# Second cross attention: one burst of four value-product groups per head in place of two bursts of two

## The chip, the cores and the metric

The kernel is one program on one core of a Trainium2 chip. The metric is device time in microseconds (us), the median of the runs; lower is better. The engines are TensorE (PE in the rows; its weight loads are PEld), VectorE (DVE), ScalarE (ACT), GpSimd (POOL) and SyncE (SP, which issues the DMAs).

## The reference

A two-layer perceiver block: in each layer a cross attention from 256 query rows to 4096 context rows, a self attention, and a feed-forward. The change lies in the cross attention of the second layer, with 16 heads of 16 columns and D = 256:

```python
def _L1_xattn_ref(query, key, value, mask, Wq, bq, Wk, bk, Wv, bv, Wo, bo):
    q = _split_heads(query @ Wq.T + bq)
    k = _split_heads(key @ Wk.T + bk)
    v = _split_heads(value @ Wv.T + bv)
    scores = jnp.einsum('bhqd,bhkd->bhqk', q, k) / jnp.sqrt(jnp.float32(DK))
    scores = jnp.where(mask, scores, jnp.float32(-1000000000.0))
    p = jax.nn.softmax(scores, axis=-1)
    out = jnp.einsum('bhqk,bhkd->bhqd', p, v)
    out = out.transpose(0, 2, 1, 3).reshape(query.shape[0], -1, D)
    return out @ Wo.T + bo
```

The mask is all true here, so the kernel takes its branch without masking.

## The kernel before

`stage_cross1` does this attention, from about 375 to 563 us of the span. One head follows another; `pairs_of_heads` runs heads 0 and 1 in straight code, heads 2 to 13 in a loop of six rounds of two heads, and heads 14 and 15 in straight code again. The order of each engine's work is written out by hand; semaphores tie the engines together.

A head has these kinds of work:

- **Score products** (`qk`, L1506): eight groups of four products each, keys by queries, 128x1024 per group, in two PSUM places that alternate. ScalarE takes the exponential of a group (L1412) into `probs`; a group may start when the exponential of the group two before it is done.
- **Value products** (`pv`, L1522): for each of the eight groups four float32 products that add into one PSUM bank, `ACC_BANK`. The four use 32 columns of the array each and lie side by side on the partitions 0, 32, 64 and 96. A float32 product has two records in the trace, so a group is two passes of four records. Here `pv g` is the value products of group g.
- **Block products** (`m_scores`, L1476): the same scores in the other layout, queries by keys, 16 blocks of 128x512 for the row maxima of a *later* head. VectorE reads each block with a maximum over the keys (L1631). They are numbered here M0 to M15 by their place in a head: M0 to M11 belong to the next head, M12 to M15 to the one after it.
- **Reduction** (`sel`, L1532): two small float32 products that add the four parts of the previous head's accumulator; VectorE then takes the reciprocal (L1640) and multiplies (L1642). The row maxima go through L1635 to GpSimd, come back by a turn on TensorE (`m_turn`, L1490) and are copied by ScalarE (L1424) into the score operand.

The block products share three PSUM banks with `sel`, which takes one of them once per head. So from M3 on a block product waits until VectorE has read the block three places before it:

```python
bank_before = {0: -2, 1: -1, 2: -3, 3: 0, 4: 2, 5: 3, 6: 1}.get(idx, idx - M_BANKS)
...
pe.wait_ge(s["m_read"], n_m * h + bank_before + 1)
```

VectorE's order in a head is: the reads of M0 to M11, L1635, L1640 and L1642 (which wait for `sel`), then the reads of M12 to M15. TensorE's order, from M0 on, is: M0, qk 0, M1 to M3, qk 1, M4, qk 2, M5, **pv 0 and 1**, M6, qk 3, M7 to M9, qk 4, M10, qk 5, M11, **pv 2 and 3**, `sel` of the head before, M12, qk 6, M13, qk 7, M14, M15, pv 4 and 5, `m_turn`, pv 6 and 7, then M0 of the next head. In heads 14 and 15 block products that would belong to heads past the last are left out: head 14 has no M12 to M15, head 15 none at all. Head 0 has no `sel` behind it.

Of the kernel before, what the change touches and what calls it, by code (L numbers as in the profile page):

```python
# [295 lines left out]
def transpose_rows(k, src, banks, done):  # L296

    for t in range(QT):
        for c in range(KT):
            last = k.nc.tensor.transpose(k.ps[:, banks, c * S + t * P:c * S + (t + 1) * P],  # L300
                                         src[:, t, c * P:(c + 1) * P], k.ident[:, :])
    last.then_inc(done, 1)
# [632 lines left out]
def rows_linear(k, src, n_k, w, bias, bank, done):  # L935

    t = k.nc.tensor
    for q in range(QT):
        o = k.ps[:, bank, q * D:(q + 1) * D]
        for c in range(n_k):  # L940
            last = t.matmul(o, src[:, c, q * P:(q + 1) * P], w[:, c, :], start=(c == 0),  # L941
                            stop=(bias is None and c == n_k - 1))
        if bias is not None:
            last = t.matmul(o, k.ones_row[0:1, 0:P], bias, start=False, stop=True)
    last.then_inc(done, 1)


def keep_busy(k, n, bank, cols=2 * D):

    for _ in range(n):  # L950
        k.nc.tensor.matmul(k.ps[:, bank, 0:cols], k.ones_sq[:, :], k.w1_o[:, :, :].rearrange("p t n -> p (t n)")[:, 0:cols], start=True, stop=True)  # L951
# [338 lines left out]
def stage_cross1(k):  # L1290
# [45 lines left out]
    with nc.Block() as block:  # L1336
# [98 lines left out]
        def _(pe):  # L1435
            t = nc.tensor

            def turn_first():

                for h in range(2):  # L1440
                    for q in range(QT):
                        last = t.transpose(turned(ACC_BANK)[:, (h * QT + q) * P:(h * QT + q + 1) * P],
                                           k.q_rows1[:, q * 2 + h, :], k.ident_bf[:, :])
                last.then_inc(s["q_turned"], 1)
# [12 lines left out]
            def m_scores(it, b, idx, masked, first, begin=False):  # L1457

                h = 2 * it + b
                blk, q = divmod(idx, QT)  # L1460
                quarter = idx // 4
                if idx == 0 and begin:
                    pe.wait_ge(s["q_first"], 1)
                elif idx == 0:
                    pe.wait_ge(qm_in[b], 16 * it)
                if idx % 4 == 0:
                    pe.wait_ge(k_in[b][quarter], 16 * K_LOADS1 * (it + 1))
                bank_before = {0: -2, 1: -1, 2: -3, 3: 0, 4: 2, 5: 3, 6: 1}.get(idx, idx - M_BANKS)
                if idx == 2 and not begin and not (first and b == 0):
                    pe.wait_ge(s["o_read"], h - 2)  # L1470
                elif not (begin and b == 0 and idx < 3):
                    pe.wait_ge(s["m_read"], n_m * h + bank_before + 1)
                o = k.ps[:, m_bank(m_turn_of(idx)), :]
                key0 = (blk % (m_blocks // 2)) * 512
                qs = k.q_st if first and h < 2 else k.q_m
                last = t.matmul(o, qs[0:MAXROW, b, q * P:(q + 1) * P],  # L1476
                                k.k_st[0:MAXROW, 2 * b + blk // (m_blocks // 2), key0:key0 + 512], start=True, stop=not masked)
                if masked:
                    last = t.matmul(o, k.ident_bf[:, :], k.mask_bias[:, q, blk * 512:(blk + 1) * 512], start=False, stop=True)
                last.then_inc(s["m_scores"], 1)  # L1480
# [34 lines left out]
            def pv(h, b, g, first):  # L1515
                pe.wait_ge(s["exp"], groups * h + g + 1)
                if g == 0:
                    pe.wait_ge(s["v_staged"], h + 1)
                    if not first:
                        pe.wait_ge(s["acc_copied"], h)  # L1520
                for m in range(GROUP_CH):
                    last = t.matmul(k.ps[32 * m:32 * m + 32, ACC_BANK, 0:S], k.v_st[:, b, GROUP_CH * g + m, :], probs[:, g, m, :],  # L1522
                                    start=(g == 0), stop=(g == groups - 1))
                last.then_inc(s["pv"], 1)
# [11 lines left out]
            def all_heads(masked):  # L1536
                keep_busy(k, 4, 6, D)
                pe.wait_ge(k.sem("c_aq"), 1)
                o = k.ps[:, 2, :].bitcast(BF16)
                for q in range(QT):  # L1540
                    for c in range(KT):
                        last = t.transpose(o[:, c * S + q * P:c * S + (q + 1) * P], k.a_q[:, q, c * P:(c + 1) * P], k.ident_bf[:, :])
                last.then_inc(k.sem("c_aqT_ps"), 1)
                pe.wait_ge(k.sem("c_aqT"), 1)
                rows_linear(k, k.a_qT, KT, k.w_tern, None, 3, k.sem("c_y"))
                keep_busy(k, 5, 6)
                pe.wait_ge(k.sem("c_xn"), QT)
                transpose_rows(k, k.xn, 2, k.sem("c_xnT_ps"))
                pe.wait_ge(k.sem("c_xnT"), 1)
                rows_linear(k, k.xnT, KT, k.w1_q, None, 3, k.sem("d_q"))  # L1550
                keep_busy(k, 2, 6)
                pe.wait_ge(s["rows"], 1)
                turn_first()
                for idx in range(n_m):
                    m_scores(0, 0, idx, masked, True, True)
                    if idx in (10, 13):
                        turn(2 * (idx // 3) - 6)
                        turn(2 * (idx // 3) - 5)
                for idx in range(M_AHEAD):
                    m_scores(0, 1, idx, masked, True, True)  # L1560
                pe.wait_ge(s["q_stack"], H // 4)
                m_turn(0, 0, True)

                def body(it, first, last):
                    for b in range(2):
                        h = 2 * it + b
                        behind = not (first and b == 0)
                        before = behind and not (first and b == 1)

                        def m_some(n0, n1):  # L1570
                            for x in m_beside(it, b, n0, n1, last):
                                m_scores(*x, masked, first)

                        if behind:
                            pv(h - 1, 1 - b, groups - 2, not before)
                            pv(h - 1, 1 - b, groups - 1, not before)
                        m_some(0, 1)
                        qk(it, b, 0, masked, first)
                        m_some(1, 4)
                        qk(it, b, 1, masked, first)  # L1580
                        m_some(4, 5)
                        qk(it, b, 2, masked, first)
                        m_some(5, 6)
                        pv(h, b, 0, not behind)
                        pv(h, b, 1, not behind)
                        m_some(6, 7)
                        qk(it, b, 3, masked, first)
                        m_some(7, 10)
                        qk(it, b, 4, masked, first)
                        m_some(10, 11)  # L1590
                        qk(it, b, 5, masked, first)
                        m_some(11, 12)
                        pv(h, b, 2, not behind)
                        pv(h, b, 3, not behind)
                        if behind:
                            if last and b == 1:
                                sel(h - 1, 1 - b, n_m * H, H - 2)
                            else:
                                sel(h - 1, 1 - b, n_m * (h + 1) + n_m - 2, None)
                        m_some(12, 13)  # L1600
                        qk(it, b, 6, masked, first)
                        m_some(13, 14)
                        qk(it, b, 7, masked, first)
                        m_some(14, 16)
                        pv(h, b, 4, not behind)
                        pv(h, b, 5, not behind)
                        if not (last and b == 1):
                            m_turn(*((it, 1) if b == 0 else (it + 1, 0)))

                pairs_of_heads(pe, body)  # L1610
                for g in range(groups - 2, groups):
                    pv(H - 1, 1, g, False)
                keep_busy(k, 1, 2, D)
                sel(H - 1, 1, n_m * H, H - 1)
                keep_busy(k, 1, 2, D)
# [499 lines left out]
```

## Time and profile before

| | before |
|---|---|
| median of 3 runs | 720.36 us (720.25 to 722.64) |
| profiled execution, span | 715.4 us |
| TensorE busy | 612.3 us (86%) |
| ScalarE busy | 456.7 us (64%) |
| VectorE busy | 407.2 us (57%) |
| one head of the loop, M0 to the next M0 | 11.91 us |

The span is the time from the first to the last instruction of one profiled execution; the median of the runs lies 5.0 us above it, outside the span. Busy times are shares of the whole span, over stages with different limits. Within the stage the change touches, a TensorE row's duration covers the whole flight of a product, and products overlap, so the row's start, and the distance to the next start, tells more than its busy time.

### The profile page before, as it was taken

How to read it: one execution, taken by the hardware profiler on the slowest of the kernel's cores; microseconds unless marked ns; L12 is line 12 of the kernel's file. 1: busy time of each engine (PE TensorE's matmuls, PEld its weight loads, DVE VectorE, ACT ScalarE, POOL GpSimd, SP SyncE). 2: the span in 40 equal slices, each digit the busy share in tenths (PEclk: the TensorE clock that was granted, in tenths of full speed). 3: DMA queues.
4: the chain of work that ended last, by engine and by line, in shares of the span. 5: the costliest groups of instructions: out<-in, count | busy, mean ns of one | idle time of the engine just before them, and what ended most of it. 6: DMA issues, size and time to landing. Idle time of an engine off the chain costs nothing. (4 is left out here: it accounts for less than half of the span.)

```text
span 715.4 us, 14402 instructions
## 1 busy us (share of the span) xinstructions
PE 612.3 (86%) x4946; PEld 365.9 (51%) x4946; DVE 407.2 (57%) x899; ACT 456.7 (64%) x541; POOL 67.4 (9%) x151
## 2 busy tenths in 40 slices
PE   1698858878878879795679999999999999898998
PEld 0353424444444445463435555555555575574786
DVE  6567371322223134876389898989896226645644
ACT  3889969999999994683027676767676414603111
POOL 3000101100001100101031212121211000000000
PEclk9999989999999999999789999999999999999999
DMA  5786766556534313203602333332231390000000
GB/s 133 217 241 228 215 198 194 146 182 188 155 103 113 92 44 99 66 2 110 199 3 79 84 80 83 80 84 78 83 80 29 101 297 1 2 1 1 0 1 15
DMA packets 52832, 73.46 MB, mean 103 GB/s; under 512 B 10979, under 2 KB 29731, under 8 KB 52795
## 3 DMA queue, kind: packets, MB, share of 16 engines
q1 hardware_dynamic: 52027, 72.25, 34.8%
q10 hardware_dynamic: 768, 0.73, 0.4%
q8 instruction: 23, 0.38, 0.2%
q14 instruction: 14, 0.11, 0.1%
HBM read 58.90 MB, written 12.85 MB: 100 GB/s over the span
## 5 line engine op out<-in xcount | busy, mean ns | idle before, releaser
L1631 DVE TENSOR_REDUCE sb_m_blk<-ps 128x1 f32<-128x512 f32 x256 | 159.5, 684 | 18.9 <-PE ps L1476 17.7
L1412 ACT ACTIVATE sb_probs<-ps 128x1024 f32<-128x1024 f32 x128 | 125.8, 1024 | 50.0 <-PE ps L1506 49.7
L655 ACT ACTIVATE sb_probs<-ps 128x1024 f32<-128x1024 f32 x128 | 124.0, 1016 | 15.8 <-PE ps L701 13.4
L659 ACT ACTIVATE sb_probs<-sb_probs,sb_neg_cap,sb_cap 128x4096 f32<-128x4096 f32 x32 | 121.6, 3801 | 1.1
L718 PE MATMUL ps<-sb_probs,sb_v_st 128*32 128x256 f32 x1024 | 76.5, 395 | 39.5 <-ACT sb_probs L659 36.8
L701 PE MATMUL ps<-sb_q_st,sb_k_st 112*128 112x256 bf16 x512 | 75.7, 283 | 5.8 <-DMA sb_k_st<-k_parts_l 3.6
L1506 PE MATMUL ps<-sb_q_st,sb_k_st 115*128 115x256 bf16 x512 | 76.4, 272 | 1.5 <-ACT sb_probs L1412 1.5
L1476 PE MATMUL ps<-sb_k_st,sb_q_m 96*128 96x512 bf16 x224 | 76.6, 383 | 0.0
L701 PEld LDWEIGHTS ps<-sb_q_st,sb_k_st 112*128 112x128 bf16 x512 | 46.0, 100 | 48.9 <-ACT sb_probs L655 24.1
L1522 PE MATMUL ps<-sb_probs,sb_v_st 128*32 128x256 f32 x1024 | 67.4, 384 | 0.2 <-ACT sb_probs L1412 0.2
L718 PEld LDWEIGHTS ps<-sb_probs,sb_v_st 128*32 128x32 f32 x1024 | 24.0, 110 | 68.0 <-ACT sb_probs L659 45.0
L1506 PEld LDWEIGHTS ps<-sb_q_st,sb_k_st 115*128 115x128 bf16 x512 | 48.7, 97 | 18.0 <-issue 1.4
L1522 PEld LDWEIGHTS ps<-sb_probs,sb_v_st 128*32 128x32 f32 x1024 | 31.3, 109 | 27.3 <-issue 14.3
L951 PE MATMUL ps<-sb_w_o,sb_ones_sq 128*128 128x512 f32 (+1 forms) x82 | 35.3, 566 | 11.0 <-issue 11.0
L1082 ACT ACTIVATE sb_q_all<-ps,sb_nmax 128x256 f32<-128x256 f32 (+1 forms) x72 | 31.7, 452 | 12.1 <-DVE sb_nmax L1098 12.1
L1476 PEld LDWEIGHTS ps<-sb_k_st,sb_q_m 96*128 96x128 bf16 x224 | 22.7, 101 | 30.0 <-DVE sb_m_blk L1631 17.1
L613 POOL TENSOR_TENSOR sb_v_st<-sb_v_rows,sb_keep 128x512 f32<-128x512 f32 x14 | 14.9, 1065 | 210.8 <-PE ps L718 142.6
L861 DVE RECIPROCAL sb_rec<-ps 128x2 f32<-128x2 f32 x16 | 2.7, 170 | 51.5 <-PE ps L727 51.5
L855 DVE COPY sb_acc_sb<-ps 128x256 f32<-128x256 f32 x16 | 6.8, 423 | 41.5 <-PE ps L718 41.5
L1098 DVE TENSOR_REDUCE sb_nmax<-ps 128x2 f32<-128x512 f32 (+1 forms) x36 | 22.6, 631 | 13.5 <-PE ps L1021 7.2
L1073 ACT ACTIVATE sb_q_all<-ps 128x512 f32<-128x512 f32 (+1 forms) x36 | 19.8, 551 | 15.6 <-PE ps L1034 15.4
L1929 ACT ACTIVATE sb_probs<-ps 128x512 f32<-128x512 f32 x9 | 5.4, 597 | 36.9 <-PE ps L1887 36.9
(282 smaller groups left out, 824.0 us busy)
## 6 DMA issues: line engine op xcount, KB each, us to landing
sb_k_st<-k_parts_l SPq DMA_DIRECT2D x223, 64.0 KB, 2.0
sb_k_st<-k_parts_l SPq DMA_DIRECT2D x93, 128.0 KB, 3.2
k_parts_l<-sb_v_proj SPq DMA_DIRECT2D x24, 256.0 KB
k_parts_l<-sb_early SPq DMA_DIRECT2D x48, 128.0 KB
sb_v_proj<-ctxT_blocks SPq DMA_DIRECT2D x8, 512.0 KB, 8.4
sb_early<-ctxT SPq DMA_DIRECT2D x7, 512.0 KB, 3.8
sb_v_rows<-ctx_by_pair SPq DMA_DIRECT2D x7, 512.0 KB, 4.2
sb_k_st<-k_parts_l SPq DMA_DIRECT2D x64, 32.0 KB, 1.8
```

The costliest lines, as they stand in the source:

```text
L655: a.activation(probs[:, j % 2, 4 * g:4 * g + 4, :], scores_bank(g), ACT.Tanh).then_inc(s["tanh"], 1)
L659: a.activation(probs[:, j % 2], probs[:, j % 2], ACT.Exp, bias=k.neg_cap[:, 0:1], scale=k.cap[:, 0:1]).then_inc(s["exp"], 1)
L701: last = t.matmul(out[:, c, :], k.k_st[0:STACK0, j, n * P:(n + 1) * P], k.q_st[0:STACK0, j // 2, :], start=True, stop=True)
L718: last = t.matmul(k.ps[32 * m:32 * m + 32, 4 + b, 0:S], k.v_st[:, b, (j % 2) * UNIT_CH + ch, :], probs[:, j % 2, ch, :], start=(j % 2 == 0 ...
L951: k.nc.tensor.matmul(k.ps[:, bank, 0:cols], k.ones_sq[:, :], k.w1_o[:, :, :].rearrange("p t n -> p (t n)")[:, 0:cols], start=True, stop=True)
L1082: sc.activation(k.sp_rows[:, n % 2, e, 0:nk], a.scores(n)[:, e, 0:nk], ACT.Exp, bias=k.nmax[:, 2 * n + e:2 * n + e + 1], accum_out=k.sums[ ...
L1098: v.tensor_reduce(k.nmax[:, 2 * n:2 * n + 2], a.scores(n)[:, :, 0:nk], AX.X, ALU.max, negate=True).then_inc(s["max"], 1)
L1412: sc.activation(probs[:, g], scores_bank(g), ACT.Exp).then_inc(s["exp"], 1)
L1476: last = t.matmul(o, qs[0:MAXROW, b, q * P:(q + 1) * P], k.k_st[0:MAXROW, 2 * b + blk // (m_blocks // 2), key0:key0 + 512], start=True, st ...
L1506: last = t.matmul(out[:, c, :], k.k_st[0:STACK, j, ch * P:(ch + 1) * P], k.q_st[0:STACK, b, :], start=True, stop=not masked)
L1522: last = t.matmul(k.ps[32 * m:32 * m + 32, ACC_BANK, 0:S], k.v_st[:, b, GROUP_CH * g + m, :], probs[:, g, m, :], start=(g == 0), stop=(g = ...
L1631: v.tensor_reduce(k.m_blk[:, b, q, blk:blk + 1], k.ps[:, m_bank(m_turn_of(idx)), :], AX.X, ALU.max).then_inc(s["m_read"], 1)
```

## The change

The value products of groups 0 and 1 leave their place between M5 and M6 and stand ahead of those of groups 2 and 3, between M11 and `sel`. M6 follows M5 directly. Nothing is added or taken away, and no wait is written differently.

```diff
                         qk(it, b, 2, masked, first)
-                        m_some(5, 6)
-                        pv(h, b, 0, not behind)
-                        pv(h, b, 1, not behind)
-                        m_some(6, 7)
+                        m_some(5, 7)
                         qk(it, b, 3, masked, first)
                         m_some(7, 10)
                         qk(it, b, 4, masked, first)
                         m_some(10, 11)
                         qk(it, b, 5, masked, first)
                         m_some(11, 12)
-                        pv(h, b, 2, not behind)
-                        pv(h, b, 3, not behind)
+                        for g in range(4):
+                            pv(h, b, g, not behind)
                         if behind:
```

In program order on TensorE, head 14 of before, from M4 on (L1476 is a block product, L1506 a score product, L1522 a value product; x8 is two groups). The heads of the loop have the same sequence with register instructions between:

```order
L1476 MATMUL ps<-sb_k_st,sb_q_m 128x512
L1506 MATMUL ps<-sb_q_st,sb_k_st 128x256 x4
L1476 MATMUL ps<-sb_k_st,sb_q_m 128x512
L1522 MATMUL ps<-sb_probs,sb_v_st 32x256 x8
L1476 MATMUL ps<-sb_k_st,sb_q_m 128x512
L1506 MATMUL ps<-sb_q_st,sb_k_st 128x256 x4
L1476 MATMUL ps<-sb_k_st,sb_q_m 128x512 x3
```

The same place, changed, from qk 1 on:

```order
L1506 MATMUL ps<-sb_q_st,sb_k_st 128x256 x4
L1476 MATMUL ps<-sb_k_st,sb_q_m 128x512
L1506 MATMUL ps<-sb_q_st,sb_k_st 128x256 x4
L1476 MATMUL ps<-sb_k_st,sb_q_m 128x512 x2
L1506 MATMUL ps<-sb_q_st,sb_k_st 128x256 x4
L1476 MATMUL ps<-sb_k_st,sb_q_m 128x512 x3
```

The value products between M5 and M6 are gone; M5 and M6 are neighbours. Later in the same head, before, from qk 4 to `sel` (L1532):

```order
L1506 MATMUL ps<-sb_q_st,sb_k_st 128x256 x4
L1476 MATMUL ps<-sb_k_st,sb_q_m 128x512
L1506 MATMUL ps<-sb_q_st,sb_k_st 128x256 x4
L1476 MATMUL ps<-sb_k_st,sb_q_m 128x512
L1522 MATMUL ps<-sb_probs,sb_v_st 32x256 x8
L1532 MATMUL ps<-sb_quad_sum,sb_acc_sb 128x32 x2
```

And changed:

```order
L1506 MATMUL ps<-sb_q_st,sb_k_st 128x256 x4
L1476 MATMUL ps<-sb_k_st,sb_q_m 128x512
L1506 MATMUL ps<-sb_q_st,sb_k_st 128x256 x4
L1476 MATMUL ps<-sb_k_st,sb_q_m 128x512
L1522 MATMUL ps<-sb_probs,sb_v_st 32x256 x16
L1532 MATMUL ps<-sb_quad_sum,sb_acc_sb 128x32 x2
```

All four groups now stand between M11 and `sel`. VectorE's order is the same in both kernels.

## Rows read from the trace of the kernel before

**Rows 1.** The page, part 1: busy us and share of each engine.

```profile
PE 612.3 (86%) x4946; PEld 365.9 (51%) x4946; DVE 407.2 (57%) x899; ACT 456.7 (64%) x541; POOL 67.4 (9%) x151
```

**Rows 2.** Stretches: length, busy of PE, PEld, DVE, ACT, POOL; clock, DMA share, GB/s.

```profile
469.82:481.73 11.91, 11.91 (x119) 6.63 (x119) 10.46 (x19) 8.41 (x10) 1.81 (x6) 1.00 0.32 82
...
20.00:35.00 15.00, 9.57 (x85) 5.66 (x84) 6.46 (x10) 12.04 (x8) 0.00 (x0) 1.00 0.88 243
```

**Rows 3.** Waits, heads 2 to 13: who for whom: us, times, longest.

```profile
PEld ps L1476 <- DVE sb_m_blk L1631: 14.7, 36, 0.4
DVE sb_m_blk L1631 <- PE ps L1476: 13.2, 12, 1.2
```

**Rows 4.** TensorE's timeline over one head: start us, us, instruction, count.

```profile
469.82 0.39 PE L1476 MATMUL ps<-sb_k_st,sb_q_m 96*128 96x512 bf16 x1
...
472.32 0.38 PE L1476 MATMUL ps<-sb_k_st,sb_q_m 96*128 96x512 bf16 x1
472.63 1.07 PE L1522 MATMUL ps<-sb_probs,sb_v_st 128*32 128x256 f32 x16
473.63 0.39 PE L1476 MATMUL ps<-sb_k_st,sb_q_m 96*128 96x512 bf16 x1
473.86 0.60 PE L1506 MATMUL ps<-sb_q_st,sb_k_st 115*128 115x256 bf16 x4
474.30 0.90 PE L1476 MATMUL ps<-sb_k_st,sb_q_m 96*128 96x512 bf16 x3
...
475.48 0.38 PE L1476 MATMUL ps<-sb_k_st,sb_q_m 96*128 96x512 bf16 x1
...
476.13 0.38 PE L1476 MATMUL ps<-sb_k_st,sb_q_m 96*128 96x512 bf16 x1
476.44 1.07 PE L1522 MATMUL ps<-sb_probs,sb_v_st 128*32 128x256 f32 x16
477.44 0.63 PE L1532 MATMUL ps<-sb_quad_sum,sb_acc_sb 128*128 128x32 f32 x4
...
479.75 1.28 PE L1522 MATMUL ps<-sb_probs,sb_v_st 128*32 128x256 f32 x19
...
481.73 0.39 PE L1476 MATMUL ps<-sb_k_st,sb_q_m 96*128 96x512 bf16 x1
```

**Rows 5.** The same timeline in narrow stretches: second and fourth pass of a burst.

```profile
472.87 0.61 PE L1522 MATMUL ps<-sb_probs,sb_v_st 128*32 128x256 f32 x8
...
473.30 0.40 PE L1522 MATMUL ps<-sb_probs,sb_v_st 128*32 128x256 f32 x4
```

**Rows 6.** Timeline of the weight loads: M9's, with its idle time and releaser.

```profile
474.81 0.10 PEld L1476 LDWEIGHTS ps<-sb_k_st,sb_q_m 96*128 96x128 bf16 x1 [0.41 <-DVE sb_m_blk L1631]
```

**Rows 7.** VectorE's timeline, the head's twelve reads, and from narrow stretches single starts.

```profile
470.25 7.55 DVE L1631 TENSOR_REDUCE sb_m_blk<-ps 128x1 f32<-128x512 f32 x12 [1.10 <-PE ps L1476]
...
472.11 1.28 DVE L1631 TENSOR_REDUCE sb_m_blk<-ps 128x1 f32<-128x512 f32 x2
472.71 1.28 DVE L1631 TENSOR_REDUCE sb_m_blk<-ps 128x1 f32<-128x512 f32 x2
...
474.06 0.69 DVE L1631 TENSOR_REDUCE sb_m_blk<-ps 128x1 f32<-128x512 f32 x1
474.72 1.29 DVE L1631 TENSOR_REDUCE sb_m_blk<-ps 128x1 f32<-128x512 f32 x2
...
478.12 0.17 DVE L1640 RECIPROCAL sb_rec<-ps 128x2 f32<-128x2 f32 x1
```

**Rows 8.** Timelines of ScalarE and TensorE in the last head, head 15.

```profile
554.48 1.95 ACT L1412 ACTIVATE sb_probs<-ps 128x1024 f32<-128x1024 f32 x2
...
557.86 0.61 PE L1506 MATMUL ps<-sb_q_st,sb_k_st 115*128 115x256 bf16 x4 [0.68 <-ACT sb_probs L1412]
558.40 1.07 PE L1522 MATMUL ps<-sb_probs,sb_v_st 128*32 128x256 f32 x16
559.40 0.63 PE L1532 MATMUL ps<-sb_quad_sum,sb_acc_sb 128*128 128x32 f32 x4
```

## The prediction, made before the changed kernel was run

> **What bounds the kernel now.** I read the page first, then the stretch of one head, then its waits, then the timelines of TensorE and VectorE side by side. The page gives TensorE as the busiest engine [rows 1], and the stretch of one head goes further: TensorE busy for all of its 11.91 us, VectorE for 10.46, ScalarE for 8.41, at a granted clock of 1.00 [rows 2]. The reader should not stop there. A product's row covers its flight, so short waits between products vanish in it, and VectorE at 88% is close enough to matter by stretches. The waits show both engines held by each other in every head: the weight loads of the block products wait for VectorE's reads 36 times in twelve heads, and VectorE waits for a block product once per head [rows 3].
>
> The timelines say where. VectorE reads M0 to M11 in one run of 7.55 us without an idle gap that the row shows, from 470.25 to 477.80, and the only long idle time, 1.10 us, lies ahead of it, while TensorE works on the value products of groups 4 to 7 [rows 7, 4]. So a head has two parts. From M0 to `sel` (469.82 to 477.44, 7.62 us) TensorE hands out blocks and VectorE reads them at 0.60 us each (472.11, 472.71): TensorE can be at most three blocks ahead, because there are three banks. From `sel` to the next M0 (477.44 to 481.73, 4.29 us) TensorE works at its own pace and VectorE has time over [rows 4, 7].
>
> In the first part TensorE has little time over today. M9 is the block where it can be seen: M7 starts at 474.30, and with the spacing of two block products, 0.22 us (0.23 from M6 to the score product behind it), M9 would start at 474.74; its weights are loaded at 474.81, released by VectorE [rows 4, 6]. That is 0.07 us. It fits the read of M6, which starts at 474.06 and takes 0.69: 474.75, and 0.06 us more to reach TensorE [rows 7]. I use these 0.06 us for every such release.
>
> **What the change takes away.** A burst of value products has ends that cost time. Into the first: M5 starts at 472.32 and the burst at 472.63, 0.31 us where the next product would otherwise come after 0.22, so 0.09. The second pass starts 0.24 after the first (472.87), while the two after that take 0.43 together, 0.215 each: 0.03. Out of it: the last pass starts at 473.30 and M6 at 473.63, 0.33 where another pass would take 0.215: 0.12 [rows 4, 5]. Together 0.24 us. One burst per head less would save 0.24 x 16 = 3.8 us, if TensorE were free to use it.
>
> **What it moves.** Pv 0 and 1 leave a place where VectorE has to catch up. I walk one head with the rows' times; all up to M5 (472.32) stays as it is.
> M6: TensorE would be ready at 472.54. Its bank is that of M3, whose read starts at 472.11 and takes 0.68 (a pair of reads 1.28, less 0.60): 472.79, and 0.06: M6 starts at 472.85. Wait 0.31.
> M7: from M6 to M7, with four score products between, is 0.67 us (473.63 to 474.30): 473.52. M4's read ended at 473.39, no wait.
> M8: ready at 473.74. M5's read starts at 473.31, ends 473.99: M8 at 474.05. Wait 0.31.
> M9: ready at 474.27. M6's read now follows M5's at once: 473.91 to 474.59: M9 at 474.65. Wait 0.38, where it was 0.07.
> M10 comes 0.67 later (475.48 less 474.81), 475.32, and M11 0.65 after that, 475.97; the reads of M7 and M8 end at 475.19 and 475.79, no wait [rows 4, 6, 7].
> So with the burst of 1.00 us (472.63 to 473.63) gone from the way, M11 comes only 0.16 us earlier (it was 476.13). Behind it the burst starts after 0.31, at 476.28, with eight passes: 0.24 + 6 x 0.215 + 0.33 = 1.86. `sel` starts at 478.14 instead of 477.44: **0.70 us later**. By the other road: waits of 1.00 in place of 0.07, less the burst's ends of 0.24, is 0.69.
>
> Nothing behind `sel` gives it back. VectorE's reciprocal starts 0.68 us after `sel` (478.12) and waits for it, the reads of M12 to M15 stand behind it in VectorE's order, and TensorE's 4.29 us to the next M0 show no block product that waits [rows 4, 7]. VectorE ends the twelve reads at 477.59 instead of 477.80 (M6's at 473.91, and five more at 0.60 and 0.68 for the last) and then idles. Whoever else waits for pv 0 and 1 has time: ScalarE overwrites `probs` of group 0 only in the next head, after 482, and GpSimd waits for pv 7 alone. ScalarE's exponentials of groups 2 and 3 are done before 475, ahead of the burst. No DMA and no queue is passed.
>
> Rows at the same offsets from M0 stand in heads 2 to 13, so 12 x 0.70 = 8.4 us. In heads 1 and 14 M5 comes 0.08 later while the reads do not: 0.62 each, 1.2 us. Head 0 has no `sel`; M12 comes late instead, about 0.6. Head 15 has no blocks and is bound by ScalarE: the two exponentials from 554.48 end at 556.43, and qk 5 waits for a third; with pv 0 and 1 out of the way that one starts at 556.42, by the spacing of 0.91 to 1.02, where now the last score product of the batch waits until 557.86. Qk 5 would then start near 557.5, 0.36 earlier, and `sel` follow 0.54 + 1.86 later, at 559.9 instead of 559.40: 0.5 [rows 8]. **Sum: 8.4 + 1.2 + 0.6 + 0.5 = 10.7 us.** The profiled execution would go from 715.4 to 726.1; the median lies 5.0 us above the span, so 720.36 becomes **731.1 us**.
>
> **Bounds of what the trace does not show.** A clean burst of eight passes is not in it. From below it is the sum above, 1.86. From above it is the existing long burst of pv 4 to 7 with the turn's two products inside, 479.75 to 481.73 [rows 4]: 1.98, so 0.12 more per head, 1.9 us in all. The reads follow each other at 0.60 when the block is there, and at 0.66 behind a read that had to wait (474.06 to 474.72) [rows 7]. M9 to M11 hang on three reads; 0.06 each would be at most 0.18 per head, 2.9 us. On the other side, only M9's wait decides when M11 comes; if its release took 0 instead of 0.06, a head would gain 0.06, 1.0 us in all; and if heads 0 and 15, which I walked least closely, lost nothing, 1.1 us more. I take 0.60, 0.06 and 1.86, since these are the rows of the same instructions in the same order. With one upper bound at a time, and half a microsecond for the scatter of the median, the case by itself spans 728.5 to 734.
>
> **Rivals.**
> *TensorE keeps the saving.* If the blocks' banks were free when TensorE reaches M6, M8 and M9, only the burst's ends would count: 720.36 - 3.8 = 716.5 us, faster by 0.54%. The row for it is TensorE's full busy time beside VectorE's 10.46 of 11.91 [rows 2]. It decides at M6: M3's read would have to end by 472.48, and it ends at 472.79 in a run of reads that starts with M0's arrival and has no gap to close [rows 7]. The Trainium skill, page "TensorEngine Tiling (Array Packing)", Key Properties, says that changing the tiling mode drains the engine. The 0.24 us are how that looks here, and by that rule alone fewer switches are a gain. The same page, PSUM Bottleneck, says that tiling speeds up TensorE but not the emptying of PSUM; here the emptying is that of the untiled blocks, and by that rule the change loses. I give this rival 0.04.
> *The lost time is given back behind `sel`.* VectorE finishes M11 about 0.9 us earlier than now relative to `sel`, and if the tail of 4.29 us held a wait on the maxima's way over GpSimd and ScalarE, the head would come out at its old 11.91 us: 720.4. Against it: TensorE's rows behind `sel` follow at the spacing of their kind, and the turn inside the long burst starts without a gap [rows 4]. Half given back would be 725.7. 0.06 for no change.
> *The clock falls.* TensorE waits 0.93 us more per head. At 1.2 GHz in place of 2.4, the 7.6 us of one part of a head would take up to twice as long; in two heads that is 15 us, 746. Against it: in the first attention TensorE was busy for 9.57 of 15 us and the clock was 1.00 [rows 2]; no single wait here is over 0.4 us. 0.04.
>
> **How the numbers follow.** The forecast has 0.86, and is slower by 1.5%. About 0.5% (3.6 us) is what a measurement of this kernel can tell from no change. Faster by more than that has 0.04, the first rival; within it 0.06, the second; slower 0.90, the forecast and the clock. The range is the forecast's own, 728.5 to 734: it leaves out the rivals, 0.14, and little of its own case.
>
> **What would show it.** One head of the loop, M0 to M0, 12.6 us instead of 11.91. M6 starting about 0.53 after M5, not 0.22; M9's weight load released by VectorE with a longer idle time ahead of it. The burst behind M11 with 32 records, and from its start to `sel` 1.86 us. VectorE idle ahead of L1640, waiting for `sel`, about 1.0 us per head, where it now starts 0.3 after the last read has ended; its 1.10 us ahead of M0's read unchanged. Wrong would be: M6 at 0.22 after M5 (the banks were free), or a stretch from `sel` to M0 shorter than 4.29.

## The result

The changed kernel takes 732.51 us, median of 6 runs (731.96 to 733.28); the kernel before, run beside it, 721.86 (720.25 to 723.89). The ratio is 1.0145, 95% interval 1.0121 to 1.0169: slower by 10.65 us. The forecast was 731.1, and 10.7 slower.

| | before | changed |
|---|---|---|
| median | 721.86 us | 732.51 us |
| profiled execution, span | 715.4 us | 730.4 us |
| one head of the loop, M0 to M0 | 11.91 us | 12.60 us |
| M0 of head 1 to M0 of head 14 | 154.90 us | 163.87 us |
| head 15, first score product to `sel` | 6.75 us | 8.75 us |
| stage, first score product to last value product | 187.7 us | 199.9 us |

The spans differ by 15.0 us, more than the medians: 12.2 us lie in the stage and 2.8 us (2.05 ahead of it, 0.76 behind it) in places where both kernels are the same, which the section on the experiments takes up. The 5.0 us by which the first median of the kernel before lies above its profiled span are hardly all time outside the span. The time of that one execution is not on record, but in every run that has both, 1.7 to 3.0 us lie outside; the rest would then be that the profiled execution was a fast one.

One head of the changed kernel, in the columns of [rows 2] (length, then busy of PE, PEld, DVE, ACT, POOL; clock, DMA share, GB/s; the clock is the mean over the stretch, 1.00 being 2.4 GHz and 0.50 being 1.2 GHz):

```profile
477.29:489.89 12.60, 12.09 (x119) 6.85 (x119) 10.30 (x19) 8.31 (x10) 1.81 (x6) 1.00 0.28 77
```

TensorE has lost its unbroken busy time: 0.51 us per head are gaps now. There is one burst less, so fewer ends, and yet the head is longer; the clock is still 1.00. The waits of heads 2 to 13 answer to [rows 3]:

```profile
PEld ps L1476 <- DVE sb_m_blk L1628: 23.0, 48, 0.5
...
DVE sb_m_blk L1628 <- PE ps L1476: 13.2, 12, 1.2
DVE sb_rec L1637 <- PE ps L1532: 12.4, 12, 1.0
```

VectorE's long idle time ahead of M0's read is what it was, 13.2 us in twelve heads. New are 12 more waits of TensorE's weight loads, one more per head, and 12.4 us in which VectorE waits for `sel`, 1.03 per head. TensorE's timeline over the same head answers to [rows 4] (start, us, instruction, count):

```profile
477.29 0.39 PE L1476 MATMUL ps<-sb_k_st,sb_q_m 96*128 96x512 bf16 x1
...
479.79 0.38 PE L1476 MATMUL ps<-sb_k_st,sb_q_m 96*128 96x512 bf16 x1
480.32 0.39 PE L1476 MATMUL ps<-sb_k_st,sb_q_m 96*128 96x512 bf16 x1
480.54 0.60 PE L1506 MATMUL ps<-sb_q_st,sb_k_st 115*128 115x256 bf16 x4
480.98 0.92 PE L1476 MATMUL ps<-sb_k_st,sb_q_m 96*128 96x512 bf16 x2
482.11 0.39 PE L1476 MATMUL ps<-sb_k_st,sb_q_m 96*128 96x512 bf16 x1 [0.21 <-DVE sb_m_blk L1628]
...
482.77 0.38 PE L1476 MATMUL ps<-sb_k_st,sb_q_m 96*128 96x512 bf16 x1
...
483.43 0.38 PE L1476 MATMUL ps<-sb_k_st,sb_q_m 96*128 96x512 bf16 x1
483.74 1.93 PE L1522 MATMUL ps<-sb_probs,sb_v_st 128*32 128x256 f32 x32
485.61 0.63 PE L1532 MATMUL ps<-sb_quad_sum,sb_acc_sb 128*128 128x32 f32 x4
...
489.89 0.39 PE L1476 MATMUL ps<-sb_k_st,sb_q_m 96*128 96x512 bf16 x1
```

M5 is at 479.79 and M6, which now follows it directly, at 480.32: 0.53 later, not 0.22. The weight loads of M3, M6, M8 and M9 (answering to [rows 6]) and VectorE's rows (to [rows 7]) say why:

```profile
478.46 0.10 PEld L1476 LDWEIGHTS ps<-sb_k_st,sb_q_m 96*128 96x128 bf16 x1 [0.41 <-DVE sb_m_blk L1628]
...
480.31 0.10 PEld L1476 LDWEIGHTS ps<-sb_k_st,sb_q_m 96*128 96x128 bf16 x1 [0.50 <-DVE sb_m_blk L1628]
...
481.51 0.10 PEld L1476 LDWEIGHTS ps<-sb_k_st,sb_q_m 96*128 96x128 bf16 x1 [0.50 <-DVE sb_m_blk L1628]
482.11 0.10 PEld L1476 LDWEIGHTS ps<-sb_k_st,sb_q_m 96*128 96x128 bf16 x1 [0.50 <-DVE sb_m_blk L1628]
```

```profile
477.71 7.33 DVE L1628 TENSOR_REDUCE sb_m_blk<-ps 128x1 f32<-128x512 f32 x12 [1.10 <-PE ps L1476]
...
486.28 0.17 DVE L1637 RECIPROCAL sb_rec<-ps 128x2 f32<-128x2 f32 x1 [1.03 <-PE ps L1532]
```

Besides M3's, which waits in the kernel before too (there also with 0.41 us ahead of it), three loads of a head are released by a read, each after 0.50 us without a load. By the count of the waits only M8's is new, because M6's was put down to a read in the kernel before as well; M3's and M6's there:

```profile
471.00 0.10 PEld L1476 LDWEIGHTS ps<-sb_k_st,sb_q_m 96*128 96x128 bf16 x1 [0.41 <-DVE sb_m_blk L1631]
...
473.63 0.10 PEld L1476 LDWEIGHTS ps<-sb_k_st,sb_q_m 96*128 96x128 bf16 x1 [0.41 <-DVE sb_m_blk L1631]
```

But M6's came right behind the burst, 0.84 us after the read of M3 had ended (472.79 to 473.63): there the burst held it, and now the read does. The twelve reads shrink from 7.55 to 7.33 us, all that the earlier M6 brings; behind them VectorE stands for 1.03 us until the long burst is over and `sel` comes.

### The profile page after: what moved, and what is told of

It is laid out like the page before. It is cut to its first block and busy times, and to the rows that moved or that the text cites. A ratio compares the mean times of both kernels' runs of the same rounds, so it can differ in the third digit from the quotient of the medians.

```text
span 730.4 us, 14402 instructions
## 1 busy us (share of the span) xinstructions
PE 619.1 (85%) x4946; PEld 370.9 (51%) x4946; DVE 403.3 (55%) x899; ACT 455.0 (62%) x541; POOL 67.2 (9%) x151
## 3 DMA queue, kind: packets, MB, share of 16 engines
HBM read 58.90 MB, written 12.85 MB: 98 GB/s over the span
## 5 line engine op out<-in xcount | busy, mean ns | idle before, releaser
L1628 DVE TENSOR_REDUCE sb_m_blk<-ps 128x1 f32<-128x512 f32 x256 | 157.1, 685 | 17.8 <-PE ps L1476 17.8
L718 PE MATMUL ps<-sb_probs,sb_v_st 128*32 128x256 f32 x1024 | 75.7, 392 | 39.1 <-ACT sb_probs L659 36.7
L1476 PE MATMUL ps<-sb_k_st,sb_q_m 96*128 96x512 bf16 x224 | 80.1, 383 | 7.0 <-DVE sb_m_blk L1628 3.6
L1506 PE MATMUL ps<-sb_q_st,sb_k_st 115*128 115x256 bf16 x512 | 76.9, 273 | 1.9 <-ACT sb_probs L1412 1.9
L1522 PE MATMUL ps<-sb_probs,sb_v_st 128*32 128x256 f32 x1024 | 65.1, 388 | 0.2 <-ACT sb_probs L1412 0.2
L1506 PEld LDWEIGHTS ps<-sb_q_st,sb_k_st 115*128 115x128 bf16 x512 | 48.8, 97 | 18.6 <-issue 1.7
L718 PEld LDWEIGHTS ps<-sb_probs,sb_v_st 128*32 128x32 f32 x1024 | 23.9, 109 | 67.4 <-ACT sb_probs L659 44.9
L1522 PEld LDWEIGHTS ps<-sb_probs,sb_v_st 128*32 128x32 f32 x1024 | 33.8, 111 | 26.2 <-issue 11.0
L1476 PEld LDWEIGHTS ps<-sb_k_st,sb_q_m 96*128 96x128 bf16 x224 | 22.6, 101 | 38.7 <-DVE sb_m_blk L1628 25.6
L951 PEld LDWEIGHTS ps<-sb_w_o,sb_ones_sq 128*128 128x128 f32 x82 | 16.6, 212 | 25.4 <-issue 24.6
```

Source lines behind the costliest of these rows:

```text
L718: last = t.matmul(k.ps[32 * m:32 * m + 32, 4 + b, 0:S], k.v_st[:, b, (j % 2) * UNIT_CH + ch, :], probs[:, j % 2, ch, :], start=(j % 2 == 0 ...
L1476: last = t.matmul(o, qs[0:MAXROW, b, q * P:(q + 1) * P], k.k_st[0:MAXROW, 2 * b + blk // (m_blocks // 2), key0:key0 + 512], start=True, st ...
L1506: last = t.matmul(out[:, c, :], k.k_st[0:STACK, j, ch * P:(ch + 1) * P], k.q_st[0:STACK, b, :], start=True, stop=not masked)
L1628: v.tensor_reduce(k.m_blk[:, b, q, blk:blk + 1], k.ps[:, m_bank(m_turn_of(idx)), :], AX.X, ALU.max).then_inc(s["m_read"], 1)
```

## The experiments

The theory: three PSUM banks let TensorE be three blocks ahead; pv 0 and 1 stood where VectorE has to catch up, and moved away they uncover the waits. Rivals: the long burst costs by itself; the number and ends of the bursts decide; the times ahead of and behind the stage play in. Where a head's time is given it comes from the profile of that kernel and is the same within 0.02 us in every head of the loop, or alternates between the two values given. The single runs of the kernel before scatter more than that (715.7 to 726.4 us beside the experiments), so the ratios below are to be read with their intervals; a ratio is not always the quotient of two medians.

**The changed kernel again.** No edit.

> The changed kernel once more, for its head period and for what lies outside it. In the first profile a head of the loop took 12.60 us against 11.91, M0 of head 1 to M0 of head 14 8.97 us more, and head 15 2.0 us more in place of my 0.5, with a granted clock of 0.60 in its long burst; 2.8 us came ahead of the stage, where the code is the same. Theory: the period comes again at 12.60, the slow clock in head 15 comes again since TensorE there waits four times for an exponential, and the 2.8 us ahead of the stage do not, or come elsewhere (they are scatter of the clock in thin stretches): 10 to 12 us over the kernel before. Rival: head 15's slow clock was chance; then its first score product to sel takes about 7.3 us, not 8.75.

Median 730.40 us, ratio 1.0127 (1.0078 to 1.0176). The head takes 12.61 us, M0 of head 1 to M0 of head 14 163.89, the stage 199.9, head 15 again 8.76 us to `sel`. The first score product starts at 375.5 instead of 377.1 (375.1 in the kernel before). So what lies inside the stage came again to within 0.03 us, the slow head 15 too. Of the 2.05 us ahead of it 0.4 are left; the 0.8 behind it came again.

**Short reads, kernel before and changed kernel.** VectorE takes the maximum over 128 of a block's 512 columns.

```diff
-v.tensor_reduce(..., k.ps[:, m_bank(m_turn_of(idx)), :], AX.X, ALU.max)
+v.tensor_reduce(..., k.ps[:, m_bank(m_turn_of(idx)), 0:128], AX.X, ALU.max)
```

> The kernel before with VectorE's reads of the blocks cut from 512 to 128 columns (the maxima are then over a quarter of the keys); everything else as it was. If the reads hold TensorE only by the 0.07 us that I read at M9 and about as much at M3, a head of the loop takes about 11.75 to 11.85 us in place of 11.91, 1 to 2 us less in all. If the reads were what sets the whole head, it would be clearly shorter, about TensorE's own 11.77 or less.

> The changed kernel with the same short reads of 128 columns. Theory (the blocks' banks are what costs): the 0.69 us per head go, M6 starts 0.22 after M5. Walking on with the rows, the next thing late is the exponential: the score products of group 3 would be ready 0.44 after M5 but the exponential of group 1 lets them go 0.3 us later, and group 5 waits some 0.1 for group 3, so most of the 0.24 saved at the burst's ends is lost there: a head of 11.7 to 11.95 us, the whole kernel within 3 us of the one with short reads before, 2 us of it head 15. Rival one (TensorE alone counts): 11.53 us, 3.8 less than with short reads before. Rival two (a burst of four groups costs by itself, whatever VectorE does): 12.5 us, over 10 us more.

Before: a head takes 11.73 and 11.85 us in turn, M0 of head 1 to M0 of head 14 153.31, the stage 2.0 us less than the profile of before; median 715.81, ratio 0.9914 (0.9879 to 0.9950). Changed: 11.88 and 11.96, 154.88, median 718.72, ratio 0.9973 (0.9941 to 1.0005). The heads came as expected, and the price of the change fell from 8.97 us over thirteen heads to 1.57. Head 15 cost 0.4 us (6.75 to 7.16) where 2 were expected. The median of the first is 4 us lower than the stage explains; that part was not expected. The timeline of the changed kernel with short reads, M5 to `sel`, and its score products' weight loads:

```profile
460.48 0.60 PE L1476 MATMUL ps<-sb_k_st,sb_q_m 96*128 96x512 bf16 x2
461.21 0.61 PE L1506 MATMUL ps<-sb_q_st,sb_k_st 115*128 115x256 bf16 x4
...
463.80 1.93 PE L1522 MATMUL ps<-sb_probs,sb_v_st 128*32 128x256 f32 x32
465.66 0.63 PE L1532 MATMUL ps<-sb_quad_sum,sb_acc_sb 128*128 128x32 f32 x4
```

```profile
461.20 0.33 PEld L1506 LDWEIGHTS ps<-sb_q_st,sb_k_st 115*128 115x128 bf16 x4 [0.62 <-ACT sb_probs L1412]
...
463.04 0.22 PEld L1506 LDWEIGHTS ps<-sb_q_st,sb_k_st 115*128 115x128 bf16 x3 [0.30 <-ACT sb_probs L1412]
```

M5 and M6 stand in one row now, 0.22 apart, so the banks are no longer late. Next late is ScalarE: the score products of group 3 start 0.73 after M5 and not 0.44, released by an exponential. The long burst takes 1.86 us (1.87 in the changed kernel), so it is not what costs, and TensorE alone does not set the time either.

**Short reads and short exponentials.** In addition one of a group's four chunks goes through the exponential, the others stay stale.

```diff
-sc.activation(probs[:, g], scores_bank(g), ACT.Exp)
+sc.activation(probs[:, g, 0:1], scores_bank(g)[:, 0:1], ACT.Exp)
```

> The kernel before with VectorE's reads of 128 instead of 512 columns and ScalarE's exponentials of one of a group's four chunks (128x256 instead of 128x1024; the rest of the probabilities is stale). This takes both other engines out of TensorE's way. Expected: a head at TensorE's own pace, 11.7 to 11.8 us, and head 15 several us shorter, since the exponentials bound it.

> The changed kernel with the same short reads and short exponentials. Theory: with both waits gone the burst's ends alone are left, so the change gains what I read from the rows, 0.24 us a head: 11.5 us, 3 to 4 us less in all than with both short before. Rival (a long burst has a price of its own): no gain, or a loss.

One head of each, before first:

```profile
454.39:466.12 11.73, 11.73 (x119) 6.91 (x119) 4.76 (x19) 3.72 (x10) 1.80 (x6) 1.00 0.33 84
```

```profile
451.84:463.33 11.49, 11.49 (x120) 7.09 (x119) 4.69 (x19) 3.72 (x10) 1.81 (x6) 1.00 0.32 83
```

11.73 and 11.49 us: with both partners out of the way the change *gains* 0.24 us a head, the number read from the burst's ends. The stage is 3.8 us shorter with it (182.8 to 179.0), the medians differ by 3.1 (713.63 and 710.54; ratios 0.9852, 0.9802 to 0.9901, and 0.9832, 0.9798 to 0.9865, whose intervals overlap, so this rests on the profiles). The saving is real and was eaten. Head 15 of the first became 1.4 us shorter (6.75 to 5.34), not several.

**Same bursts, another place.** In the kernel before, pv 0 and 1 now stand between M7 and M8 (the edit is shortened here).

```diff
-m_some(5, 6); pv(h, b, 0, ...); pv(h, b, 1, ...); m_some(6, 7)
+m_some(5, 7)
 qk(it, b, 3, masked, first)
-m_some(7, 10)
+m_some(7, 8); pv(h, b, 0, ...); pv(h, b, 1, ...); m_some(8, 10)
```

> The kernel before, with pv 0 and 1 two steps later (between M7 and M8, behind qk 3) and not merged: as many bursts as before, of the same size, with the same products between. If the number and the ends of the bursts decided, nothing would change: 11.91 us a head. Theory (M6 waits for M3's read): walking with the rows, M6 starts 0.31 late, the burst of 1.00 behind M7 then covers the waits of M8 and M9, M11 starts 0.24 later than before, and a head takes 12.15 us, 3 to 3.5 us more in all.

12.15 us a head, M0 of head 1 to M0 of head 14 157.88, 3.0 us over before. Its timeline from M5:

```profile
466.39 0.38 PE L1476 MATMUL ps<-sb_k_st,sb_q_m 96*128 96x512 bf16 x1
466.93 0.39 PE L1476 MATMUL ps<-sb_k_st,sb_q_m 96*128 96x512 bf16 x1 [0.15 <-DVE sb_m_blk L1631]
...
467.59 0.38 PE L1476 MATMUL ps<-sb_k_st,sb_q_m 96*128 96x512 bf16 x1
467.90 1.07 PE L1522 MATMUL ps<-sb_probs,sb_v_st 128*32 128x256 f32 x16
468.90 0.61 PE L1476 MATMUL ps<-sb_k_st,sb_q_m 96*128 96x512 bf16 x2
...
471.75 0.63 PE L1532 MATMUL ps<-sb_quad_sum,sb_acc_sb 128*128 128x32 f32 x4
```

M6 waits as in the changed kernel (0.54 behind M5), M8 and M9 do not: the burst covers them. Not the number of bursts but what they cover decides. The timing does not show the 3 us: median 723.32 against 721.29, ratio 0.9998 (0.9971 to 1.0024). By profile the expectation held, by the timing it did not. Head 15 came out shorter in this order than in either other, 6.44 us to `sel` at a clock of 1.00, against 6.75 before; a kernel with this order in head 15 alone was not run.

**Head 15.** Four kernels. The changed one with the old order in head 15 alone; the one before with the new order there alone; that one with three idle products in the gaps; and the changed one with them. An idle product is one into a free bank whose result nobody reads. Of the idle products the edit shows the first.

```diff
 qk(it, b, 2, masked, first)      # head 15 alone; another keep_busy behind qk 3 and qk 4
+pe.wait_ge(s["m_read"], n_m * H); keep_busy(k, 1, 6, D)
```

> The changed kernel, but head 15 in the old order (pv 0 and 1 behind group 2). Theory: head 15's thin stretch, in which TensorE waits for ScalarE and has no value products to do, is what brings the clock down to 1.2 GHz for the burst behind it; with the old order the clock stays at 1.00 there and head 15 takes 6.75 us from its first score product to sel, not 8.75: 2 us less than the changed kernel, head period still 12.60. Rival (the slow clock was chance): the same as the changed kernel within 0.5 us.

> The kernel before, with the new order in head 15 alone. Theory: head 15 has no blocks, so what it loses it loses by waiting for ScalarE and by the clock: from its first score product to sel 8.75 us with a stretch at 1.2 GHz, as in the changed kernel twice, against 6.75; or 7.15, as with the short reads, if the clock holds. Everything ahead of it as before, 11.91 us a head. In all 0.4 to 2 us more, too little for the timing; the profile decides. Rival (head 15's price comes from the heads ahead of it, which wait for VectorE): 6.75 us.

> The kernel before with the new order in head 15 alone, and there one idle product of 256 float32 columns into a free bank behind each of the score products of groups 2, 3 and 4, in the time in which TensorE waits for an exponential. Theory: the clock fell in head 15 (three of three full-length runs with the new order there) because TensorE had so little to do; with the gaps filled the granted clock stays at 1.00 through the burst and head 15 takes 7.1 to 7.5 us from its first score product to sel. Rival (the long burst itself, or the place, brings the clock down): a stretch at 1.2 GHz again and 8.7 us or more.

> The changed kernel with the three idle products in head 15, a second sample of the filled gaps, now behind fifteen heads of the new order. Theory: clock 1.00 through head 15's burst, 7.2 us from its first score product to sel, 1.55 less than in the changed kernel twice; a head of the loop 12.60 us as there. Rival: it falls here too, 8.7 us.

| kernel | order in head 15 | first score product to `sel` | clock, mean |
|---|---|---|---|
| before, first profile | old | 6.75 us | 1.00 |
| old order in head 15 alone | old | 6.76 us | 1.00 |
| changed, first and second profile | new | 8.75, 8.76 | 0.80, 0.81 |
| before with new head 15 | new | 8.76 | 0.81 |
| before with new head 15, gaps filled | new | 7.19 | 1.00 |
| changed, gaps filled | new | 7.19 | 1.00 |
| changed, short reads | new | 7.16 | 1.00 |

The timeline of head 15 in the changed kernel answers to [rows 8], and three stretches of it, the last across the other two, show the clock:

```profile
566.73 0.60 PE L1506 MATMUL ps<-sb_q_st,sb_k_st 115*128 115x256 bf16 x4 [0.77 <-ACT sb_probs L1412]
567.83 0.61 PE L1506 MATMUL ps<-sb_q_st,sb_k_st 115*128 115x256 bf16 x4 [0.51 <-ACT sb_probs L1412]
568.84 0.60 PE L1506 MATMUL ps<-sb_q_st,sb_k_st 115*128 115x256 bf16 x4 [0.40 <-ACT sb_probs L1412]
569.66 1.03 PE L1506 MATMUL ps<-sb_q_st,sb_k_st 115*128 115x256 bf16 x4 [0.23 <-ACT sb_probs L1412]
570.63 3.10 PE L1522 MATMUL ps<-sb_probs,sb_v_st 128*32 128x256 f32 x32
573.66 0.63 PE L1532 MATMUL ps<-sb_quad_sum,sb_acc_sb 128*128 128x32 f32 x4
```

```profile
566.73:570.63 3.90, 2.77 (x17) 1.35 (x17) 0.00 (x0) 3.79 (x5) 0.00 (x0) 0.87 0.00 0
570.63:573.66 3.03, 3.03 (x34) 1.31 (x33) 0.00 (x0) 1.02 (x1) 0.00 (x0) 0.60 0.02 5
569.70:573.00 3.30, 3.30 (x28) 1.58 (x32) 0.00 (x0) 1.85 (x2) 0.00 (x0) 0.50 0.02 5
```

The long burst takes 3.03 us where it takes 1.87 in the heads ahead; from 569.70 to 573.00 the clock is 0.50, 1.2 GHz. Its second pass starts at 571.06, 0.43 us after the first:

```profile
571.06 1.07 PE L1522 MATMUL ps<-sb_probs,sb_v_st 128*32 128x256 f32 x7
```

TensorE had waited for an exponential ahead of four groups of score products; the value products that used to stand between them had been its work. The kernel before with the new order in head 15 alone has the same 8.76 us, so the heads ahead of it are not the cause. With the gaps filled by idle products (in the kernel before with the new head 15) the same burst runs at full clock:

```profile
550.55:555.88 5.33, 4.49 (x35) 2.90 (x31) 0.00 (x0) 4.68 (x6) 0.00 (x0) 1.00 0.00 0
555.88:557.74 1.86, 1.86 (x33) 0.93 (x32) 0.00 (x0) 1.20 (x2) 0.00 (x0) 1.00 0.04 9
```

That makes the order worth 0.4 us (6.76 to 7.19) and the clock 1.57. In three unfilled profiles the clock fell, in two filled ones it did not. In the fourth unfilled one, with short reads, it did not fall either, though its gaps in head 15 are the same. So the burst itself is not the cause, and the gaps do not always suffice; that they are needed is likely, but two filled profiles do not prove it, and what else it takes was not found. The kernel before with the new head 15 has a ratio of 1.0020 (0.9988 to 1.0052): too little for the timing, as expected. The filled kernels were timed once each, 718.66 us against 716.27 for the kernel before beside it, and 726.76 against 719.26, with 12.60 us a head in the second as expected. The old order in head 15 alone took 6.76 us there, but its stage came out at 199.8 us, no shorter than the changed kernel's, because head 0 ran 1.9 us longer at a low clock; its median of 730.52 shows no gain.

**The kernel before again.**

> The kernel before once more, for its profile. The stage took 12.2 us more in two profiles of the changed kernel, the medians differ by 8 to 11 us. If the first profile of before is typical, its stage takes 187.7 us again from the first score product to the last value product, 6.75 of it head 15's first part; if its stage has slow stretches in other executions, it takes a few us more, and that is what the medians have less.

One run, 718.32 us, against 719.26 beside it. The loop is the same (11.91 us a head, M0 of head 1 to M0 of head 14 154.88, head 15 6.76), but the stage takes 190.35 us, 2.7 more than in the first profile (187.68). All of it is head 0; first product to M0 of head 1, again and then in the first profile:

```profile
372.91:386.89 13.98, 13.98 (x114) 7.28 (x113) 10.41 (x18) 8.35 (x9) 1.20 (x5) 0.79 0.23 64
```

```profile
375.08:386.38 11.30, 11.30 (x115) 6.24 (x113) 10.32 (x18) 8.24 (x9) 1.20 (x5) 1.00 0.25 70
```

At the start of the stage the clock is 1.00 in one execution and 0.79 in another. Against this profile the change costs 9.5 us in the stage, against the first 12.2; the medians give 10.65 and 8.4. Which is typical two profiles cannot say, but the thirteen of this document together say more: head 0 is at full clock in eight of them and below it in five (0.78 to 0.88). Among the five are heads in the old order (this one, and the kernel before with the filled head 15: 12.73 us in place of 11.30) and in the new one (the changed kernel with the old head 15: 13.80 in place of 11.92, and with the filled one: 12.85). So the slow start comes in both orders and is no price of the change. A part of up to 4 us between medians and profiles stays open.

## Why the prediction was right

*The bound.* Right. The forecast read a head as two parts, one at VectorE's pace and one at TensorE's own. The part behind `sel` stayed 4.28 us (485.61 to 489.89; it was 4.29 by [rows 4]); all of the loss lies ahead of it. With short reads it all but disappears.

*The walk.* Right to 0.01 us per step. Measured from M0, the forecast and the changed kernel: M6 3.03 and 3.03, M8 4.23 and 4.22, M9 4.83 and 4.82, M11 6.15 and 6.14, `sel` 8.32 and 8.32. The head is 12.60 instead of 11.91, 0.69 to 0.70 more.

*What the burst's ends save.* 0.24 us forecast, 0.24 measured where nothing else waits (11.73 to 11.49). The Trainium skill, page "TensorEngine Tiling (Array Packing)", Key Properties, says that a change of the tiling mode drains TensorE; the 0.24 us agree with that, but no run tells a drain from other costs at a burst's ends. What the same page of the Trainium skill says under PSUM Bottleneck, that tiling does not speed up the emptying of PSUM, no run here tests, since none changes the tiling. The saving counts where TensorE has nothing to wait for.

*The unknown size.* The clean burst of eight passes took 1.87 us, the lower bound of 1.86 to 1.98. The reads followed at 0.60.

*Heads 0, 1 and 14.* Forecast 0.6, 0.62 and 0.62; measured, from their first product or M0 on, 0.61 to 0.62 (11.92 for 11.30; 12.60 for 11.99; 11.99 for 11.37).

*Head 15.* Mis-sized: 0.5 forecast, 2.0 measured. What the order alone costs was near: with the clock up `sel` comes 0.41 to 0.44 later, and qk 5 starts 0.46 earlier in the changed kernel (569.66, 4.75 behind the first score product, in place of 5.21) where the walk had 0.36. Missing is the slow clock, 1.6 us. The rival on the clock had the mechanism, but looked for it in the heads that wait for VectorE, where no wait is over 0.4 us, and not in head 15, which I had described as bound by ScalarE without asking what the gaps do to the clock.

*The sum.* 8.4 + 1.2 + 0.6 + 0.5 = 10.7 forecast; 12.2 by the first two profiles, of which 1.6 is head 15's clock. The median's 10.65 agrees with the forecast more closely than its terms do, and that is luck: the 1.6 us that the forecast missed are offset by something that the medians hold and the first two profiles do not, probably executions of the kernel before that are slower than its first profile, as the second one is with head 0 at a low clock. The 5.0 us between median and span that I added are no constant of the kernel: in the profiled run of the changed kernel, run and span differ by 1.7 us (732.11 and 730.4). The upper end of the range also leaves out the half microsecond that the text adds (731.1 + 2.9 + 0.5 is 734.5, not 734); the result lies inside either.

*The rivals.* "TensorE keeps the saving" is true only with both partners shortened. "Given back behind `sel`" did not happen. What would show the steps came as listed: 12.6, 0.53, 32 records, 1.87, about 1.0 us of waiting for `sel`, and the 1.10 ahead of M0 unchanged.

None of the kernels that do the whole work beats the one before.

## What to carry to other kernels

A burst moved out of the way is not only work moved: ask what it covered, by walking the partner's timeline step by step from where it stood. A saving at a burst's ends, here 0.24 us, counts only if no partner engine is within that much of being late, and the next one (here ScalarE behind VectorE) may be just as near. In a stretch that waits for another engine, small products between the waits may be what keeps TensorE's clock.

## What the runs showed of the hardware

TensorE's clock fell to 1.2 GHz in head 15 in three of four profiles, though no single gap there was over 0.77 us; value-product passes then started 0.43 us apart in place of 0.215 (the burst took 3.03 us in place of 1.87). In both profiles with three idle products in the gaps it stayed at 2.4. The Trainium skill, page "TensorE: Matmul & The Clock Gate", Part 1, says that the slow clock is the default and that activity releases it; these profiles agree with that. In stretches that are the same in both kernels the clock differed from one execution to the next, worth 2.7 us at the start of this stage alone, so that two profiles of one kernel can differ by as much as a small change is worth, while the heads of the loop repeat to 0.02 us.
